# Second half's convolutions in 32 by 32 tiles of the matmul array, with the context added in the copies, and two roundings on other engines

## What is computed

```
x = x + _L0_ffn_ref(_L0_cond_ref(x, cond_128, L0_cond_weight, L0_cond_c_weight, fside_S_0), ...)
x = x + _L1_ffn_ref(_L1_cond_ref(x, cond_128, L1_cond_W0, ...), ...)

# _L0_cond_ref: 9 taps, 4 groups of 8 channels, plus one value per sample and channel
out = lax.conv_general_dilated(x, weight, window_strides=(STRIDE,), padding=[(PAD, PAD)], dimension_numbers=('NCH', 'OIH', 'NCH'), feature_group_count=GROUPS)
ctx = jnp.einsum('nd,od->no', c, c_weight)
out = out + ctx[:, :, None] + bias[None, :, None]
# _L0_ffn_ref
logits = jnp.einsum('bsh,he->bse', hidden_states, gate_w)
routing_weights, selected_experts = jax.lax.top_k(logits, K)
h = jax.nn.relu(jnp.einsum('bsh,hi->bsi', hidden_states, up_w)) ** 2
shared_out = jnp.einsum('bsi,ih->bsh', h, down_w)
x_latent = jnp.einsum('bsh,hl->bsl', hidden_states, fc1_w)
expert_out = jnp.einsum('bsl,lm->bsm', x_latent, expert_w)
moe_out = expert_out * jnp.sum(routing_weights, axis=-1, keepdims=True)
routed_out = jnp.einsum('bsl,lh->bsh', moe_out, fc2_w)
return _layernorm(shared_out + routed_out, ln_gamma, ln_beta)
```

## Time and profile before

| | us |
|---|---|
| runs | 221.25, 217.3, 221.2 (median 221.2) |
| the profiled execution, its own time | 217.51 |
| its span in the trace | 215.7 |

### The profile page before, as it was taken

One profiled execution on the slowest core, in us unless ns is written; L12 is line 12 of the kernel. 1 busy time (PEld: TensorE's weight loads), 2 busy tenths in 40 slices (PEclk: granted clock), 3 DMA queues, 4 the chain that ended last, 5 costly groups with the idle time before them and its releaser, 6 DMA issues.

```text
span 215.7 us, 3106 instructions
## 1 busy us (share of the span) xinstructions
PE 211.2 (98%) x1155; PEld 183.4 (85%) x1155; DVE 124.8 (58%) x265; ACT 80.1 (37%) x156; POOL 61.8 (29%) x77
## 2 busy tenths in 40 slices
PE   7999899999999999999999999999999999999994
PEld 7997778888887789987888888888998998999984
DVE  4979356869525455597852034456996537435443
ACT  5998555369384612222222034431013112121110
POOL 3018421340475620021960012442264202202000
PEclk9999999999999999999999999999999999999999
DMA  6999655310000000174645000000000110110104
GB/s 177 346 406 406 219 116 109 61 27 0 0 3 0 0 0 3 25 123 68 91 41 146 0 0 0 3 0 2 0 3 0 49 49 3 50 49 0 52 0 146
DMA packets 31455, 14.94 MB, mean 69 GB/s; under 512 B 25336, under 2 KB 26168, under 8 KB 31440
## 3 DMA queue, kind: packets, MB, share of 16 engines
q1 hardware_dynamic: 30624, 14.05, 23.4%
q10 hardware_dynamic: 816, 0.69, 1.5%
HBM read 12.62 MB, written 2.11 MB: 68 GB/s over the span
## 4 chain that ended last, share of the span: by engine, by line
PE 95%; DVE 4%; issue 0%; DVEq 0%
PE PS L1214 26%; PE PS L1216 25%; PE PS L1215 25%; PE PS L1233 9%; PE PS L1341 3%; PE PS L1403 2%; DVE up_lo L864 1%; DVE H_lo L885 1%; PE PS L1258 1%; PE PS L1257 1%; PE PS L1412 1%; PE PS L1370 0%; PE PS L1267 0%; DVE ex_lo L997 0%; DVE up_hi L993 0%; PE PS L1456 0%
## 5 line engine op out<-in xcount | busy, mean ns | idle before, releaser
L910 DVE TENSOR_TENSOR PS<-PS,relu 128x512 f32<-128x512 f32 x16 | 11.2, 699 | 30.9 <-ACT relu L675 30.9
L1214 PE MATMUL PS<-H_hi,up_hi 128*128 128x512 f32 x64 | 25.6, 399 | 0.5 <-DVE H_lo L885 0.5
L1216 PE MATMUL PS<-H_hi,up_lo 128*128 128x512 f32 x64 | 25.0, 390 | 0.0
L1215 PE MATMUL PS<-H_lo,up_hi 128*128 128x512 f32 x64 | 25.0, 390 | 0.0
L1233 PE MATMUL PS<-wconv,XS 128*128 128x128 f32 x192 | 22.4, 276 | 0.0
L1233 PEld LDWEIGHTS PS<-wconv,XS 128*128 128x128 f32 x192 | 21.9, 192 | 0.3
L1216 PE MATMUL PS<-qkT_hi,H_lo 128*128 128x320 f32 x64 | 19.8, 309 | 0.0
L1215 PE MATMUL PS<-qkT_lo,H_hi 128*128 128x320 f32 x64 | 19.8, 309 | 0.0
L1214 PE MATMUL PS<-qkT_hi,H_hi 128*128 128x320 f32 x64 | 19.7, 308 | 0.0
L675 ACT ACTIVATE relu<-PS 128x512 f32<-128x512 f32 x16 | 9.5, 594 | 25.5 <-PE PS L1216 23.0
L595 POOL TENSOR_TENSOR X<-X,rowb 128x512 f32<-128x512 f32 x8 | 10.3, 1297 | 28.1 <-PE PS L1341 28.1
(11 more groups left out here) (187 smaller groups left out, 459.6 us busy)
## 6 DMA issues: line engine op xcount, KB each, us to landing
up_raw<-in_L_ffn_up_w_dram SPq DMA_DIRECT2D x2, 1024.0 KB, 8.9
dn_raw<-in_L_ffn_down_w_dram SPq DMA_DIRECT2D x2, 1024.0 KB, 13.0
out_dram<-X SPq DMA_DIRECT2D x7, 256.0 KB, 2.0
X<-in_x_dram SPq DMA_DIRECT2D x1, 1024.0 KB, 13.9
XS<-in_L_ffn_W_dram SPq DMA_DIRECT2D x16, 64.0 KB, 2.3
X<-in_x_dram SPq DMA_DIRECT2D x2, 256.0 KB, 2.9
X<-in_x_dram SPq DMA_DIRECT2D x1, 512.0 KB, 5.4
fc<-in_L_ffn_fc_w_dram SPq DMA_DIRECT2D x1, 512.0 KB, 5.7
```

The source lines that it names most:

```text
L910: nc.vector.tensor_tensor(U[i % 2], U[i % 2], relu[:], ALU.mult).then_inc(s_sq, 1)
L1214: nc.tensor.matmul(o, lh, rh, start=start, stop=False)
L1215: nc.tensor.matmul(o, lh, rl, start=False, stop=False)
L1216: return nc.tensor.matmul(o, ll, rh, start=False, stop=stop)
```

## The change

In the second half each group of 8 channels is convolved by itself. A group's 8 channels by 4 phases are 32 rows; 16 samples are dealt to 4 columns of tiles. So there are 3 windows by 4 by 4 = 48 matmuls with a stationary tile of 32 by 32 and 512 moving columns (`group_convs`). Their output has channels and phases on the partitions and positions in the columns; ACT (group 0) and DVE (groups 1 to 3) copy it to `wide` in SBUF and add the context value on the way, and 16 PE transposes (`turn_groups`) turn it into tokens in PSUM. `split_H` then reads PSUM directly. `XS` is refilled for it by DMA: ACT and DVE pick the phases with two copies each over all partitions into `wide`, 4 DMAs write them to `xph_rows` in DRAM, 16 DMAs read them back by group. The weights are picked from `wconv` by 16 DMAs and put in order by one POOL copy. The memory of `wide` is that of `B1` and `BD`, so BD is now zeroed after the second half's convolutions.

On PE, the steps of the small network stand one chunk earlier, and `down(6)` stands behind the group matmuls. In the opening `fc2` is rounded by DVE, the row values by ACT, and POOL makes a reordered copy `rows_p`.

```diff
-    ctx_rows = nc.dram_tensor("ctx_rows", [N // 2, C], F32, kind="Internal").ap()
+    ctx_rows = nc.dram_tensor("ctx_rows", [TPH * CG, SPT * G], F32, kind="Internal").ap()
+    xph_rows = nc.dram_tensor("xph_rows", [PH, C, SPT, TPH, P], F32, kind="Internal").ap()
...
@@ SP
-            sp.wait_ge(s_ctx, 1)
-            sp.dma_start(ctx_rows, rows[N // 2:N]).then_inc(s_ctxw, 16)
+            sp.wait_ge(s_rowsp, 1)
+            for t in range(TPH):
+                sp.dma_start(ctx_rows[CG * t:CG * (t + 1)].rearrange("o (s g) -> s o g", g=G),
...
+            sp.wait_ge(s_wconv, NWIN)
+            for g in range(G):
+                for j in range(PH):
+                    sp.dma_start(wgrp[C * g + CG * j:C * g + CG * (j + 1)].rearrange("k a (p o) -> k (a p) o", o=CG),
...
+            sp.wait_ge(xs_v, 10)
+            sp.wait_ge(xs_a, 7)
+            for s in range(SPT):
+                sp.dma_start(xph_rows[:, :, s].rearrange("j c t m -> c j (t m)"), wide[C * s:C * (s + 1)])\
+                    .then_inc(s_xpw, 16)
+            sp.wait_ge(s_xpw, 16 * SPT)
+            sp.wait_ge(s_conv, TPH)
+            for g in range(G):
+                for j in range(PH):
+                    sp.dma_start(XS[C * g + CG * j:C * g + CG * (j + 1), :, 1:1 + P],
+                                 xph_rows[j, CG * g:CG * (g + 1)].rearrange("c s t m -> c (s t) m")).then_inc(ld_xs, 16)
...
@@ POOL, opening
+            pool.wait_ge(s_ctx, 1)
+            nc.gpsimd.tensor_copy(rows_p[:].rearrange("n (o g) -> n g o", g=G),
+                                  rows[0:N].rearrange("n (g o) -> n g o", g=G)).then_inc(s_rowsp, 1)
...
-            nc.gpsimd.memset(BD[:], 0.0).then_inc(s_zero, 1)
...
@@ POOL, behind the loop over the first half's chunks
+            pool.wait_ge(ld_wgrp, 16 * G * PH)
+            nc.gpsimd.tensor_copy(wgrp_op.rearrange("k a (o p) -> k a p o", p=PH),
+                                  wgrp.rearrange("k a (p o) -> k a p o", p=PH)).then_inc(s_wgrp, 1)
             for T in range(TPH):
                 norm_scale(T)
+            pool.wait_ge(s_conv, TILES)
+            nc.gpsimd.memset(BD, 0.0).then_inc(s_zero, 1)
...
@@ ACT
-            act.wait_ge(ld_fc2, 16)
-            nc.scalar.activation(fc2_hi, fc2[:], ACT.Copy).then_inc(s_fc2h, 1)
...
+            act.wait_ge(s_ctx, 1)
+            nc.scalar.activation(rows_hl[:], rows[:], ACT.Copy).then_inc(s_ctx, 1)
...
+                    act.wait_ge(s_grp, 1)
+                    act.wait_ge(s_B0, 16)
+                    for s in range(SPT):
+                        nc.scalar.activation(wide[:, 0, s * P:(s + 1) * P], conv_bank(TPH)[:, s * P:(s + 1) * P],
+                                             ACT.Identity, bias=bctx[:, s, 0:1]).then_inc(s_ga, 1)
...
-                        if c in (5, 6):
-                            hidden(c - 5)
-                        if c == 7:
-                            exp_att()
+                        if c in (4, 5):
+                            hidden(c - 4)
                     up_relu(i0 + c)
                     up_split(i0 + c)
...
+                    if h == 0 and c == 4:
+                        split_wk()
                     if h == 0 and c == 5:
-                        split_wk()
-                    if h == 0 and c == IC - 1:
+                        exp_att()
+                    if h == 0 and c == 6:
                         copy_attT()
...
@@ DVE
+            dve.wait_ge(ld_fc2, 16)
+            nc.vector.tensor_copy(fc2_hi, fc2[:]).then_inc(s_fc2h, 1)
...
-            nc.vector.tensor_copy(rows_hl[:], rows[:]).then_inc(s_ctx, 1)
...
+                    dve.wait_ge(s_grp, 1)
+                    dve.wait_ge(s_B0, 16)
+                    for g in range(1, G):
+                        nc.vector.tensor_tensor(wide[:, g].rearrange("q (s m) -> q s m", s=SPT),
+                                                conv_bank(TPH + g).rearrange("q (s m) -> q s m", s=SPT),
+                                                bctx[:, :, g].unsqueeze(2).broadcast_to([P, SPT, P]), ALU.add)\
+                            .then_inc(s_gv, 1)
...
@@ PE
+            def group_convs():
+
+                pe.wait_ge(s_wgrp, 1)
+                pe.wait_ge(ld_xs, 16 * G * PH)
+                pe.wait_ge(s_R, IC)
+                pe.wait_ge(s_lat, LC)
+                pe.wait_ge(s_agg, 2)
+                pe.wait_ge(s_aggb, 1)
+                for a in range(NWIN):
+                    for t in range(TPH):
+                        for g in range(G):
+                            gs = slice(C * g, C * (g + 1))
+                            last = nc.tensor.matmul(conv_bank(TPH + g)[C * t:C * (t + 1), :],
+                                                    wgrp_op[gs, a],
+                                                    XS[gs, :, a:a + P].rearrange("k (s t) m -> k t s m", t=TPH)[:, t],
+                                                    start=(a == 0), stop=(a == NWIN - 1))
+                last.then_inc(s_grp, 1)
+
+            def turn_groups():
+
+                pe.wait_ge(s_ga, SPT)
+                pe.wait_ge(s_gv, G - 1)
+                for s in range(SPT):
+                    view = conv_bank(TPH + s).rearrange("m (t p g o) -> m g t o p", p=PH, g=G, o=CG)
+                    for g in range(G):
+                        last = nc.tensor.transpose(view[:, g], wide[:, g, s * P:(s + 1) * P], ident[:])
                     last.then_inc(s_conv, 1)
...
-                    conv(TPH)
-                    for t in range(1, TPH):
-                        conv(TPH + t)
+                    group_convs()
+                    down(IC - 2)
+                    turn_groups()
                     down(IC - 1)
...
-                for c in range(IC if h else IC - 1):
+                for c in range(IC if h else IC - 2):
                     down(h * IC + c)
                     if c == 1:
                         routed(h)
-                    if h == 0:
-                        conditioning(c)
+                    if h == 0 and c == 1:
+                        cond_layer0()
+                    if h == 0 and c == 2:
+                        cond_layer1()
+                    if h == 0 and c == 4:
+                        mixing()
                     if c + 3 < IC:
                         up(h * IC + c + 3)
+                    if h == 0 and c == 2:
+                        cond_logits()
+                    if h == 0 and c == 3:
+                        turn_att()
```

More of the change, by code:

```diff
@@ L143, in bass_adaln_ffn @@
         rowb = sb("rowb", [P, L])
-        B0 = sb("B0", [P, TOKH])
-        B1 = sb("B1", [P, N * C])
-        BD = sb("BD", [P, TILES, P])
+        small = sb("small", [P, TOKH])
+        wgrp, wgrp_op = (small[:, b * P:b * P + NWIN * C].rearrange("k (a q) -> k a q", a=NWIN) for b in range(2))
+        bctx = small[:, 2 * P:2 * P + SPT * G].rearrange("q (s g) -> q s g", s=SPT)
+        big = sb("big", [P, 2, N * C])
+        B1 = big[:, 0]
+        BD = big[:, 1].rearrange("p (t q) -> p t q", q=P)
+        wide = big[:].rearrange("p a (t l) -> p (a t) l", l=L)
         H_hi = sb("H_hi", [P, PH, TOKH], F32R)
@@ L1449, in mixing @@
                 pe.wait_ge(s_aTl, 1)
[L1450 to L1452 removed]
+                nc.tensor.matmul(M[0][N:2 * N, 0:C], attT2[:], bk[:], start=True, stop=True).then_inc(s_aggbp, 1)
                 pe.wait_ge(s_wk, 1)
```

124 lines of the change are left out of this document (58 added, 66 removed).

## The result

The changed kernel took 219.38 us (median of 20 executions, 216.9 to 220.73), the kernel before, beside it, 217.59 (216.99 to 222.25). The ratio is 1.0074, its 95% interval 1.0052 to 1.0095: slower, by less than 2%. (The ratio compares the faster group of executions of each kernel; eight of the twenty of the kernel before lie apart, at 221.2 to 222.3.) I had named 219.5 us, but as 1.7 us *less* than the median of the three runs shown (221.2); against 217.6 my change would have given 215.9. The number came out by luck, the sign was wrong.

What follows compares the result with a forecast made beforehand. PE's instruction list, one after the other, was taken as the bound. PE's list -6.0, logits +1.7, mixing +0.1, `s_wgrp` +3.1 and opening -0.6 sum to -1.7 us: 219.5 us from a median of 221.2, range 215 to 238.

Steps and rivals of the forecast that it cites:

- Conv block removed: PE's 48 convolution matmuls of the second half go away: -10.7 us.
- transposes: 16 PE transposes of 128 by 128 added behind the group matmuls: +1.8 us.
- logits: New PE wait at cond_logits behind up(5), for hidden(1) from ACT: +1.7 us, bounds 1.2 and 2.2.
- mixing: PE's wait at mixing for the transposed softmax weights split by ACT and DVE: +0.1 us, up to 1.0.
- covers of the context adds and of the split of `H`: DVE's context adds (2.1 us) and the H_hi/H_lo split (about 4.0) hide under PE work; a failure costs at most 1 us.
- All 16 tiles side by side: Group block: 48 small matmuls run 16 at once, three rounds of 0.89 us, +2.7 us; chance 0.50.
- Records that block the queue: Rival: in the group block a matmul's second record holds back the next tile; block 21.4 us, total +17; chance 0.34.
- `s_wgrp` late, +3.1: PE waits before the group matmuls for POOL's weight copy, queued behind group_split(3): +3.1 us, bounds 2.6 and 3.5.
- if PE does not wait for `s_wgrp`: Named sign that the prediction is wrong: no PE wait for POOL's weight copy, expected at about 3.1 us.
- The data of `XS` ... 10 us of room: Second half's refill by DMA lands near 68 us, needed at about 78, so no wait.
- Opening, -0.6: Before up(0): rounding moved between engines and an earlier fc2_lo on POOL gain 0.6 us, bounds -0.7 and +0.3.
- The clock falls in the stall, +1.5: Rival: PE works some 3 us at doubled matmul price behind the 3.1 us stall, +1.5 us, 221; no chance of its own.

Runs made afterwards that it cites:

- experiment 3: Changed kernel with POOL's copy of the group weights ahead of split_dn(5) and XS refilled by 4 DMAs instead of 16; 216.24 us, ratio 0.9916.
- experiment 8: experiment 3 with the 48 group matmuls reordered, the three taps of one tile one behind the other; 229.25 us, ratio 1.055.
- experiment 2: Changed kernel with XS refilled by 4 DMAs of 32 partitions instead of 16 of 8; 219.01 us, ratio 1.0068.
- experiment 7: experiment 3 plus the opening as before the change and the rounding of wk moved early; 214.77 us, ratio 0.9895.
- experiment 1: Changed kernel with only POOL's copy of the group weights moved ahead of split_dn(5); 217.62 us, ratio 1.0006.
- 5: experiment 3 with the opening as before the change: fc2_hi back on ACT, all of rows_hl back on DVE; 214.36 us, ratio 0.9857.
- 9: experiment 7 with the four writes of the second half's data issued ahead of 12 of the 16 loads of Wk; 217.39 us, ratio 0.9968.

## Why the prediction was wrong

- *Conv block removed, transposes, logits, mixing, covers of the context adds and of the split of `H`*: right, each to about 0.1 us. No wait for `H_lo` stands ahead of `up(8)`.
- *All 16 tiles side by side*: right, and the row that I took for a matmul of 512 columns (four times that of 128) was the right one: two records of 0.43 each. Three matmuls a tile are six rounds of records, 2.6 us; the block took 3.40. In experiment 3 the rounds start 0.43, 0.62, 0.46, 0.62 and 0.46 us apart, and the last ends 0.82 us behind its start. The term was short by 0.7, and by another 1.4 where the clock fell behind the stall. By the factor in "TensorE: Matmul & The Clock Gate", part 3, of the Trainium skill, whose row for 16 tiles names no number of columns, I had an estimate of 4.0; the measured 3.40 is below it.
- *Records that block the queue*: refuted as I had put it, by the sixteen records that start within 0.11 us. A related blocking, by the next matmul of a busy tile, exists (experiment 8); the order of the loops kept it out. The trace of before could show neither.
- *`s_wgrp` late, +3.1*: mechanism and size right (2.9 by the end of the copy in the changed kernel, 2.97 in experiment 2), the place in the sum wrong: in the profiled execution a longer wait covered it, which is the sign of being wrong that I had named ("if PE does not wait for `s_wgrp`").
- **The step that failed:** "The data of `XS` ... 10 us of room". I had them at 68 us; they were in at 82.0. Of the 14 us, 3.2 are the arrival of SP at the writes (56.2 instead of 53: the gathers cost 11.89 us, not 8.2, since an issue of this shape takes 0.7 us and not the 0.51 of the earlier trace rows); 1.9 are the issues of writes and reads (1.7 + 10.4 instead of 10.2); 8.9 are the two landings, for which 4.8 us remain in my sum, from no row, and which took 4.3 and 9.4. My wait of 3.1 us became 4.2, and with it came the clock's 1.4: 2.5 of the 3.8 us between -1.7 and +2.1. Without them this execution would have come out 0.4 us faster than before. The group block's own 0.7 and the opening's 0.8 are most of the rest. In the executions of the changed kernel that stayed at full clock the step may not have counted, since POOL's copy may have held PE there (experiment 3).
- *Opening, -0.6*: wrong in sign, +0.16 in the profiled execution, 0.8 us of the miss; and +0.69 from `rows` to `up(0)`, where the moment of the start doesn't enter, so the term itself was off by 1.3. I let POOL's subtraction start 0.4 us earlier than 16.02 and counted only what that frees behind it; it started at 15.03 and came to lie beside the 32 by 32 subtraction, which is on the path. Undoing it brought the way from `rows` to `up(0)` back to 7.25 us in experiment 7.
- *The clock falls in the stall, +1.5*: this rival came true with its size, 1.4, in the profiled execution. Seven of the twenty executions have a mean granted clock under 1.000 and thirteen don't, so it isn't part of the median.

What stays open: what sets the moment at which the clock is full and PE's rate doubles in the opening; why two of the changed kernel's executions are as fast as 216.9; and why the kernel before has executions near 217.2 and near 221.2, 4 us apart, where the versions here are 2.1 apart.

## What to carry to other kernels

Before a change that adds transfers to a queue, write down that queue's whole list with a price for each issue from a row of the same shape (few partitions, short packets) and a landing for each dependent pair, as one does for PE; the transfer with room is the one for which both are known. A wait in a profile names one releaser and hides a second that is nearly as late: look up in its own timeline when each was done, and repair both. And when an engine's path gets shorter, ask which chain that doesn't depend on it now comes last.

## What the runs showed of the hardware

- Sixteen 32 by 32 tiles work at once with plain float32: 48 matmuls of 512 columns in 3.40 us in an order where no tile is given its next matmul before the others have theirs; 16.1 us with three in a row on one tile.
- POOL beside DVE: 32 by 32 from 0.18 to 2.24 and 2.46 us, ending with POOL's. In run 7 the fold (0.68, two inputs in SBUF) had started 0.25 us ahead of POOL's subtraction and wasn't stretched, nor was the one of `ex` (0.69, one input in PSUM); the two `up_lo` behind it took 2.78 instead of 1.4. So a start 0.25 us ahead of POOL's was enough; one 0.08 us ahead, in 5 and in 9, was not, and the 32 by 32 subtraction was held for 2.46 us all the same. With the opening as it was before the change only late starts had the collision, with the changed opening both.
- The granted clock fell with stalls of PE of 2.8 and 4.2 us (0.7 to 1.6 us after PE had resumed; at half for 3.4 us) and of 3.3, 3.4 and 4.7 us (while PE still stood; at half for 6.8 us), and not with stalls of 2.7 and 3.0.
- The same 512 B packets took 2.3 times the engines' time in transfers that fill 8 partitions as in those that fill 32 (44.2% in experiment 1 against 19.5% in experiment 2).
